# Mixing tiles of a cross-attention and stream-mixing kernel: placed behind every second step of the queries, instead of behind every fourth step of the whole order

## What is computed

```python
# layer 1, per batch: linear cross-attention over the layer norm of x
q = Wq @ layernorm(x); k = Wk @ ctx; v = Wv @ ctx      # 512 x 2048, 8 heads of 64
q = softmax(q, over the 64 of a head) * 64**-0.5
k = softmax(k, over the 2048 columns)
out = Wo @ (per head: (k v^T)^T q) + bo
x = x + out / norm(out, over the 256 rows) * g * 16

# layer 2, per row (a "token" of 4 streams of 512 columns), on the layer norm of x
H_res  = sinkhorn(4 x 4 logits of the token, 50 iterations)
H_pre, H_post = softmax(4 logits), softmax(4 logits)
y   = (sum of the 4 streams by H_pre) @ W_branch
x   = x + H_res' @ streams + outer(H_post, y)
```

## Time and profile before

| what | us |
|---|---|
| median of 3 runs | 2837.36 (2836.42 to 2837.56) |
| profiled execution | 2838.41, its span 2836.7 |
| PE busy, of the span | 2528.3 (89%) |
| DVE busy | 1715.8 (60%) |
| ACT busy | 1103.8 (39%) |
| POOL busy | 921.2 (32%) |
| mean granted PE clock | 0.961 |

### The profile page before, as it was taken

How to read it: one execution, slowest core, us unless ns; L and a number is a source line. 1 busy time by engine, 2 the same in 40 slices (tenths; PEclk the granted TensorE clock), 3 DMA queues, 4 the chain that set the end, 5 groups by cost and what they waited for, 6 DMA issues and landing times.

```text
span 2836.7 us, 34124 instructions
## 1 busy us (share of the span) xinstructions
PE 2528.3 (89%) x11492; PEld 1838.4 (65%) x11492; DVE 1715.8 (60%) x4226; ACT 1103.8 (39%) x2374; POOL 921.2 (32%) x870
## 2 busy tenths in 40 slices
PE   6989899999989899998989989898998989989853
PEld 5777777777666677666667666666766667666510
DVE  2444534446766757455674867634687685876685
ACT  2434334434333333434334343343433334343322
POOL 2433415060513315061340605224062250521412
PEclk9999999999999999999999999999999999999976
DMA  6112121212112121423323222232323414231254
GB/s 214 45 64 93 60 90 45 94 40 97 52 56 93 60 82 38 136 78 108 123 75 120 84 91 69 84 125 68 126 78 106 124 49 139 77 107 36 80 164 136
DMA packets 200140, 255.65 MB, mean 90 GB/s; under 512 B 43550, under 2 KB 109854, under 8 KB 199966
## 3 DMA queue, kind: packets, MB, share of 16 engines
q1 hardware_dynamic: 199966, 253.47, 28.4%
HBM read 177.53 MB, written 75.89 MB: 89 GB/s over the span
## 4 chain that ended last, share of the span: by engine, by line
PE 72%; DVE 17%; ACT 3%; issue 3%; POOL 2%; DMA 1%; SPq 0%; DVEq 0%; POOLq 0%; ACTq 0%
PE big L666 15%; PE kc_bank L609 15%; PE big L641 13%; PE tb L651 4%; PE tb L708 4%; PE tb L595 3%; PE big L583 3%; PE big L585 3%; PE big L584 3%; PE tb L719 3%; PE misc L688 3%; DVE stats L838 2%; ACT turned L1199 2%; PE kc_bank L685 1%; DVE ska L1015 1%
## 5 line engine op out<-in xcount | busy, mean ns | idle before, releaser
L1199 ACT COPY turned<-tb 128x512 f32<-128x512 f32 x512 | 297.6, 586 | 937.0 <-PE tb L651 660.0
L666 PE MATMUL big<-merged,turned 128*128 128x256 f32 x2048 | 492.9, 383 | 62.4 <-ACT turned L1199 61.0
L609 PE MATMUL kc_bank<-ctxt,turned 128*128 128x256 f32 x2048 | 492.2, 385 | 32.5 <-ACT turned L1199 32.5
L666 PEld LDWEIGHTS big<-merged,turned 128*128 128x128 f32 x2048 | 380.9, 190 | 207.8 <-issue 124.8
L641 PE MATMUL big<-wq,x_sb 128*128 128x512 f32 x1024 | 486.5, 600 | 5.9 <-DVE q_sb L908 5.1
L609 PEld LDWEIGHTS kc_bank<-ctxt,turned 128*128 128x128 f32 x2048 | 379.0, 194 | 89.4 <-issue 46.4
L1414 POOL TENSOR_TENSOR ctx_l<-stage,ctx_h 128x512 fp32r<-128x512 f32 x128 | 164.1, 1283 | 602.5 <-ACT ctx_h L1234 602.5
L1444 POOL TENSOR_TENSOR q_sb<-q_sb,qsum 128x1024 f32<-128x1024 f32 x128 | 243.4, 1901 | 272.8 <-DVE qsum L920 272.8
L811 DVE TENSOR_REDUCE kmax<-big 128x1 f32<-128x512 f32 x256 | 174.6, 686 | 225.9 <-PE big L585 224.9
L719 PE MATMUL tb<-mix_ld,mix_w 121*96 121x512 f32 (+2 forms) x324 | 192.0, 692 | 105.1 <-POOL mix_w L1426 85.6
L641 PEld LDWEIGHTS big<-wq,x_sb 128*128 128x128 f32 x1024 | 181.5, 192 | 157.4 <-issue 146.8
(11 more groups left out here) (137 smaller groups left out, 3692.8 us busy)
## 6 DMA issues: line engine op xcount, KB each, us to landing
mix_ld<-streams SPq DMA_DIRECT2D x157, 240.0 KB
stage<-in_ctx SPq DMA_DIRECT2D x64, 512.0 KB, 5.8
ctxt<-in_ctx_t SPq DMA_DIRECT2D x64, 512.0 KB, 6.4
x_sb<-in_x SPq DMA_DIRECT2D x64, 512.0 KB, 6.3
x_tr<-in_x_t SPq DMA_DIRECT2D x64, 512.0 KB, 6.7
streams<-x_sb SPq DMA_DIRECT2D x64, 512.0 KB, 2.8
out<-mix_out SPq DMA_DIRECT2D x157, 192.0 KB, 2.2
streams<-y_sb SPq DMA_DIRECT2D x32, 256.0 KB, 2.0
```

The source lines that it names most:

```text
L609: t = nc.tensor.matmul(kc_bank[:, 0:C], turned[n % 3][:, j * P:(j + 1) * P], ctxt[:, nt, :], start=nt == 0, stop=nt == NT - 1)
L666: t = nc.tensor.matmul(big[2 + p % 2][:, half], turned[n % 3][:, dt * P:(dt + 1) * P], merged[:, dt, :], start=dt == 0, stop=dt == DT - 1)
L1199: nc.scalar.copy(turned[k % 3][:], tb[n % 2][:]).then_inc(s_tba, 1)
```

## The change

The count of places now runs over the places of the queries alone, and a tile is put where it reaches 2 instead of 4. No tile is put in the keys. The pause behind a group's coefficients stays at `since` = -2.

```diff
-    PACE = 4
+    PACE = 2
...
-            since = min(since, PACE - 6)
+            since = min(since, PACE - 4)
+        if place[0] != "Q":
+            continue
         since += 1
         if mixed < loaded and since >= PACE:
             put_mix(place)
             since = 0
```

## The result

| what | before | changed |
|---|---|---|
| median of 13 runs, us | 2836.33 (2832.19 to 2838.46) | 2848.45 (2837.10 to 2850.32) |
| ratio to before | | 1.0037 (95% interval 1.0026 to 1.0048) |
| span of the profiled execution | 2836.7 | 2844.7 |
| PE / DVE / ACT / POOL busy | 2528.3 / 1715.8 / 1103.8 / 921.2 | 2530.5 / 1705.3 / 1104.5 / 919.0 |
| mean granted PE clock | 0.961 | 0.961 |

The change makes the kernel slower by 0.37%, some 10 us by the ratio and 12 by the medians. Ten of the 13 runs took 2846 to 2850, at a mean granted clock of 0.957 to 0.961, and three 2837 to 2841 at 0.962 to 0.964; no profile of a short one exists, so what sets them apart stays open.

What follows compares the result with a forecast made beforehand. PE was taken as the bound, 72% of the chain; -8.6 - 19.8 - 6.0 + 31.0 - 1.7 = -5.1 us put the profiled execution at 2833.3 and the median at 2832.3, range 2819 to 2849.

Steps and rivals of the forecast that it cites:

- part 4: Queries: 36 costing tiles become 72, at 0.86 us each +31.0 us; batch 13 hides two, -1.7.
- Parts 1 to 3: Keys without tiles: batches 7 and 11 -8.6 us; 8, 12 and 14 -19.8; 9, 13 and 15 -6.0.
- part 2: Keys of batches 8, 12, 14: seam's wait for late weights goes, 6.6 us less each, -19.8 in all.
- Part 5: Tail: six more tiles under the last Sinkhorn, 44 instead of 38, cost 0, bounds 0 and +3 us.
- Part 6: Transfers and GpSimd: counts unchanged, loads still led by some 25 us in the queries; 0.
- Rival A: Queries: ScalarE's queue makes dense tiles dear; slower, median 2846 at half price, 2860 at full; chance 0.20.
- B: Queries with Sinkhorn steps: denser tiles fill half their 4.2 us of waits; faster, median 2818; chance 0.13.
- C: Keys: lower clock without tiles takes the seams' gain, 2.0 us each in batches 8, 12, 14; median 2838; chance 0.09.
- part 3: Keys of batches 9, 13, 15, mid-group, likened to batch 6: 2.0 us less each, -6.0; batch 10: 0.

Runs made afterwards that it cites:

- e3_weights: Kernel before the change, with tiles' weights made one tile further ahead (mixed + 3 instead of mixed + 2): 2838.16 us, ratio 1.0004 to before.
- e5_tile_first: Changed kernel, same tiles, but at query places 2, 3 and 4 the tile runs ahead of chain steps and transposes, banks rotating accordingly: 2833.10 us, ratio 0.9986 to before.
- e1_odd: Changed kernel with tiles only at odd places of the queries, 103 instead of 107 ahead of the tail: 2822.16 us, ratio 0.9944 to before.
- e6_late_dense: Changed kernel with query tiles at 1, 3, 5, 9, 14 to 19, 25 (11 too from batch 11), weights one tile further ahead, `since` capped: 2797.11 us, ratio 0.9857 to before.
- e2_even: Changed kernel with tiles only at even places of the queries, 105 ahead of the tail: 2855.62 us, ratio 1.0063 to before.
- e4_late: Changed kernel without tiles at query places 0 to 5, 95 ahead of the tail and 56 under its Sinkhorn: 2837.35 us, ratio 0.9997 to before.
- c_after: The changed kernel run again, unmodified, beside later experiments on the same chip: 2848.31 us, ratio 1.0038 to before.

## Why the prediction was wrong

It said 2832.3, within 0.2% of before with a lean to faster; the median was 2848.45, at the very top of its range, and slower. The step that failed is part 4, the price of 0.86 us for a tile at every place of the queries.

- **Parts 1 to 3, the keys: -34.4 forecast, -32.8 measured.** Batches 7 and 11 gave 4.2 and 4.3 (forecast 4.3). Batch 8 gave 7.8, 12 gave 5.3 and 14 gave 3.6 (6.6 each; 16.7 of 19.8). Batches 9, 13 and 15 gave 2.1, 0.6 and 5.2 (2.0 each), batch 10 took 0.3. In sum, taking batches without tiles as likes was sound; batch by batch it missed by up to 3.2 us either way, and that the misses cancel is luck.
- **The cause named in part 2 was wrong.** PE's 4.81 us for `mix_w` looked like the cost of the seam. `e3_weights` took that wait away and nothing came back, since `k_exp` was as late. The comparison with a seam without tiles stopped too early: it read 0.94 us, and 15 us further on PE stands another 8.37 us in that same seam, before its first `key_context`:

```profile
984.62 1.62 PE L609 MATMUL kc_bank<-ctxt,turned 128*128 128x256 f32 x3 [8.37 <-ACT turned L1199]
```

  The sum was near because it was read from batch 4 and not from that wait. Most of what the keys gave was the tiles' own PE time behind the seam. Cut at the end of round 0's last `key_context`, the rest of the keys gave 25.3 of the 32.8 us, 3.9 of them in batch 8 and 3.6 in batch 9, for four tiles each. The stretch from the last `return_pair` to that cut went its own way: 26.9 to 23.0 in batch 8, but 26.2 to 27.6 in batch 9 and 30.6 to 33.1 in batch 13, longer with fewer tiles. Why it differs is open.
- **Part 4, the queries: +29.3 forecast, +44.1 measured. This is the step that failed**, in "36 that cost became 72, and 36 x 0.86". The price of 0.86 holds in the middle, and six places at the end are free, as it said. But it was taken for all places, and the early ones had been seen only with tiles four places apart. At places 2 and 4 a tile takes a bank that VectorE reads one place later. The four batches with tiles there (8, 10, 12 and 15) took 13.6 of the 14.8 us over the forecast. In batch 10 places 2 and 3 took 10.9 us with the tile, against 7.9 in `e5_tile_first` with the same tile; that reordering took 4.7 us out of batch 8's queries, 4.4 out of batch 10's, and in all it gave back 15 us, as much as the miss in the queries. It could have been read beforehand: line 1159 says when VectorE reads, and the trace of the kernel before has the wait already, 6.7 us of it, with 1.73, 1.64 and 2.82 us at place 2 of batches 9, 13 and 15:

```profile
L719 PE MATMUL tb<-mix_ld,mix_w 121*96 121x512 f32 x314 | 185.0, 688 | 96.8 <-POOL mix_w L1426 77.2 <-ACT mix_out L1262 12.0 <-DVE merged L807 6.7
```

  A lone tile there did not show the price: places 2 to 5 took 15.8 us in batch 9 with one tile and 14.9 in batch 10 with none, 0.9 apart.
- **The clock is part of that price.** The granted clock of the queries is 0.97 or 0.98 in five batches now (7, 8, 10, 12 and 15) and was in three before (8, 13 and 15); in `e1_odd` it is in one and in `e6_late_dense` in none. What one such fall costs varies: batch 7, with the same tiles, took 104.3 here at 0.98 and 102.7 in `e1_odd` at 1.00, and batch 8 took 102.1 before at 0.98 and in `e3_weights` at 1.00.
- **Batch 7** took 104.3 (forecast 100.9; part 4's own term, three more tiles on 99.8, makes it 102.4), batch 11, built alike, 102.6. In both PE waited 1.95 us for the weights of a group's first tile, made in its own place, at place 3; in batch 7 the slower clock behind it cost the rest.
- **Part 5: 0 forecast, -1.4 measured. Part 6: 0**, and no wait for a load shows in the queries.
- **Rival A** had the right sign and the wrong mechanism, so that its 2846 at half the price is near by luck: it wanted ScalarE's copies to make every second tile dear. `e2_even` and `e4_late` exclude that in the middle of the queries; the excess sits in two places and in VectorE's read. Only at the end, at 20 and 22, a copy delays the pairs behind it, 0.8 us more than at 21 and 23. **B** did not happen. **C**: the keys of batch 8 kept 0.95 and batch 12 its 0.93, but those of 9, 10 and 13 fell from 0.95 to 0.92, 0.92 and 0.91, and those of 14 from 0.98 to 0.95; part 3 had that for 9 and 13. None of the four got longer by more than 0.3 us, and batch 7's keys took 64.4 us at 0.95 here and at 0.92 in `c_after`, so the fall is seen and its price is not. The clock also fell in a new place, behind the wait at place 2. The Trainium skill, "TensorE: Matmul & The Clock Gate", Part 1, says that the throttled state is the default and activity releases it; both falls, in the seams and behind the 3.41 us at place 2 (0.56), agree.

## What to carry to other kernels

Work put into another engine stream costs only its own time where its buffer is free, and more where it is not: when a tile joins a rotation of two banks, count the users ahead of it and look up at which point of its own program the reader empties them. Fill the waits that the trace shows one by one (here behind each transpose without logits, 0.7 us each), not at an even pace: 103 tiles, six of each batch's ten to twelve in such places, took 25 us less than 103 at the odd places. And a wait put down to one engine is its price only if no other release comes within the same few microseconds; take it away in a run of its own before counting on it.

## What was not expected of the hardware

A wait of 3.41 us in the middle of dense work was followed by a granted clock of 0.56 for 3.4 us, so that a matmul group of 1.88 us took 2.68 and a tile of 1.02 took 2.02; the wait cost more than its length. A wait of 1.95 us, at place 3 of batch 7, was followed by a fall of the clock as well, and the same wait in `e1_odd` was not.

VectorE's small Sinkhorn products took up to 1.67 us beside a GpSimd instruction and never over 0.3 without one, so GpSimd's work, 3% of the chain that ended last, can set how late VectorE empties a bank.

In the tail, SP issues the four transfers of a tile in 1.6 to 1.9 us where they follow each other densely (`e4_late`), and 48 tiles under some 104 us of Sinkhorn steps were still free while 56 made the tail 5.5 to 6.5 us longer than 48 did. That SP's issuing is what makes it longer is not shown.
